# Latent attention on one Trainium2 core: turning the probabilities on VectorE and through DRAM instead of on TensorE

## The reference, cut to what matters

```python
xn = layer_norm(x, g1, b1)
ln = layer_norm(latents, g2, b2)
q = ln @ Wq
kv_input = jnp.concatenate([xn, ln], axis=1)
kv = kv_input @ Wkv
k, v = jnp.split(kv, 2, axis=-1)
q, k, v = (heads(q), heads(k), heads(v))
scale = 1.0 / np.sqrt(np.sqrt(DIM_HEAD))
logits = jnp.einsum('bhqd,bhkd->bhqk', q * scale, k * scale)
w = jax.nn.softmax(logits.astype(jnp.float32), axis=-1).astype(logits.dtype)
out = jnp.einsum('bhqk,bhkd->bhqd', w, v)
out = out.transpose(0, 2, 1, 3).reshape(b, l, INNER)
return out @ Wout
```

## Time and profile before

| | us |
|---|---|
| median of 3 runs | 1884.95 (1884.7 to 1889.27) |
| the profiled execution | 1885.37 |
| its span, first to last instruction | 1883.6 |
| PE busy / DVE / ACT / POOL in it | 1802.6 / 1199.9 / 879.5 / 616.8 |

### The profile page before, as it was taken

The page is one execution under the profiler, slowest core; times in us unless marked ns, Lnnn a source line. Parts: engine busy times, 40 slices in busy tenths (PEclk is TensorE's granted clock), DMA queues, the critical chain, the costliest instruction groups (busy, mean ns, idle before and its releaser), DMA issues. The chain is left out here.

```text
span 1883.6 us, 49778 instructions
## 1 busy us (share of the span) xinstructions
PE 1802.6 (96%) x20072; PEld 1350.2 (72%) x20072; DVE 1199.9 (64%) x2921; ACT 879.5 (47%) x1662; POOL 616.8 (33%) x744
## 2 busy tenths in 40 slices
PE   6999999999999999999999999989988999999988
PEld 4666666667888888888756667866766788888853
DVE  6677777637676666776643222238877777777767
ACT  2444444445555555555432223337764444444445
POOL 2111111103333333433313532442321444444447
PEclk9999999999999999999999999999999999999999
DMA  9300000000000000000010001321010000000001
GB/s 320 91 2 0 0 0 0 1 1 1 1 1 0 0 0 0 0 0 0 1 78 26 26 29 64 109 66 31 22 31 14 2 3 2 2 3 3 3 7 40
DMA packets 37926, 46.16 MB, mean 25 GB/s; under 512 B 5000, under 2 KB 32443, under 8 KB 37266
## 3 DMA queue, kind: packets, MB, share of 16 engines
q1 hardware_dynamic: 34450, 38.43, 6.5%
q0 software_dynamic: 3328, 5.58, 0.9%
HBM read 28.67 MB, written 17.10 MB: 24 GB/s over the span
## 5 line engine op out<-in xcount | busy, mean ns | idle before, releaser
L154 POOL TENSOR_TENSOR rstd<-var_eps,minus_half 128x2 f32<-128x2 f32 (+1 forms) x116 | 91.9, 792 | 429.5 <-DVE var_eps L148 429.4
L1068 POOL TENSOR_TENSOR xa_probs<-xa_probs,xa_total 128x512 f32<-128x512 f32 x128 | 133.0, 1039 | 196.4 <-DVE xa_total L1109 191.7
L1114 DVE TENSOR_REDUCE xa_top<-ps 128x4 f32<-128x512 f32 x128 | 88.1, 688 | 129.7 <-PE ps L933 128.4
L1029 ACT ACTIVATE xa_probs<-xa_probs 128x512 f32<-128x512 f32 x128 | 80.8, 631 | 157.2 <-DVE xa_probs L1117 157.2
L922 PEld LDWEIGHTS ps<-xa_kvT,pack_latent 128*128 128x128 f32 x512 | 97.8, 192 | 66.1 <-issue 43.8
L933 PE MATMUL ps<-xa_kvT,xa_qT 128*128 128x128 f32 x1024 | 135.2, 275 | 0.0
L949 PE MATMUL ps<-xa_probsT,xa_kv 128*128 128x512 f32 x256 | 133.2, 602 | 1.9 <-ACT xa_attnT L1038 1.8
L922 PE MATMUL ps<-xa_kvT,pack_latent 128*128 128x256 f32 x512 | 132.2, 384 | 1.4 <-PEq L343 1.4
L395 PEld LDWEIGHTS ps<-pack_moe,la_hid 128*128 128x128 f32 x1024 | 121.0, 192 | 17.4 <-issue 15.3
L382 PE MATMUL ps<-la_h2T,pack_moe 128*128 128x512 f32 x256 | 129.9, 616 | 3.3 <-ACT la_hid L591 3.3
L395 PE MATMUL ps<-pack_moe,la_hid 128*128 128x128 f32 x1024 | 125.2, 277 | 0.0
(11 more groups left out here) (355 smaller groups left out, 3954.0 us busy)
## 6 DMA issues: line engine op xcount, KB each, us to landing
expert_weights<-experts_dram SPq DMA_DIRECT2D x8, 768.0 KB, 5.9
result_pairs<-zeros SPq DMA_DIRECT2D x1, 4096.0 KB, 29.6
ca_got<-result_pairs SPq DMA_DIRECT2D x16, 256.0 KB, 2.7
slot_rows<-zeros SPq DMA_DIRECT2D x1, 2880.0 KB, 18.4
expert_rows<-slot_rows SPq DMA_DIRECT2D x8, 360.0 KB, 3.5
pack_moe<-moe_dram SPq DMA_DIRECT2D x1, 2312.0 KB
pack_latent<-latent_dram SPq DMA_DIRECT2D x1, 2050.0 KB, 15.3
pack_latent<-biased_dram SPq DMA_DIRECT2D x1, 2048.0 KB, 8.2
```

The source lines that it names most:

```text
L154: pool.tensor_tensor(m.rstd[:, 0:tiles], m.var_eps[:, 0:tiles], m.minus_half[:, 0:tiles], ALU.pow).then_inc(sem.rstd, 1)
L1068: pool.tensor_tensor(probs[:, u % 4], probs[:, u % 4], over(total[:, u % 4], 2, KEYS), ALU.mult).then_inc(probs_ready, 1)
L1114: dve.tensor_reduce(top[:, s % 4], scores, AX.X, ALU.max).then_inc(top_ready, 1)
```

## The change

The probabilities no longer go through PE. DVE transposes each 32x32 block of the probabilities' tile into `blocks`; SP stores the tile to DRAM (`turned_blocks`) and, when it has landed, loads it back with the blocks set on the keys' partitions (`probsT`). For the load's partition order to be the natural order of the keys, the scores are computed with their key columns permuted: the moving operand of `score` reads kvT with a step of 4 elements (16 bytes). Bank 2 is free, so attended values alternate between banks 2 and 3, and attending moves from slot s-3 to s-4 behind the scores.

The subtraction of the largest score is gone: the folded weights carry the factor -1/8, DVE takes the smallest of the negated scores (which is minus the largest), and ACT computes exp(-score + smallest) from PSUM straight into `probs`, in 4 instructions of 128 columns (the bias is one number per partition and pair of heads). The output projection of tiles 0 and 1 moves from slots 7 and 3 to slots 0 and 4 of the next step.

```diff
-                def copy_fold(fold, done, ready):
+                def copy_fold(fold, done, ready, scale):
...
+                            act.activation(heads[:, g, par], tiles_of(m.bank(4 + 2 * g + par)), ACT.Copy,
+                                           scale=scale).then_inc(ready, 1)
...
+            @block.sync
+            def _(sp):
+                def spread(step, u):
+
+                    sp.wait_ge(blocks_turned, count(step, UNITS, u + 1))
+                    sp.dma_start(m.turned_blocks[u % SETS].rearrange("p (j e) -> p j e", j=QUARTERS),
+                                 blocks[:, u % SETS].rearrange("p j n q -> p j (n q)")).then_inc(blocks_stored, 16)
+                    sp.wait_ge(blocks_stored, count(step, 16 * UNITS, 16 * u + 16))
+                    sp.dma_start(probsT[:, u % SETS].rearrange("p g n q -> p g (n q)"),
+                                 m.turned_blocks[u % SETS].rearrange("(g k) (j e) -> (k j) g e", g=QUARTERS, j=QUARTERS))\
+                        .then_inc(probsT_loaded[u % SETS], 16)
...
                     pe.wait_ge(q_ready, count(step, PROJ, UP * half + UP))
+                    reach(pe, exp_ready, count(step, UNITS, u - 1))
...
-                                       kvT[:, k, seq, :], start=True, stop=True)
+                                       kvT[:, k, seq, :].rearrange("p (k j) -> p j k", j=QUARTERS), start=True, stop=True)
...
-                def turn(step, u):
-                    reach(pe, probs_ready, count(step, UNITS, u + 1))
-                    reach(pe, probsT_ready, count(step, UNITS, u))
-                    for n in range(UP):
-                        mm = pe.transpose(bank(TURN_BANK)[:, P * n:P * n + P], probs[:, u % 4, n, :], w["ident"][:])
-                    mm.then_inc(probs_turned, 1)
...
+                    pe.wait_ge(probsT_loaded[u % SETS], count(step, 16 * UNITS // SETS, 16 * (u // SETS + 1)))
+                    reach(pe, attn_ready, count(step, UNITS, u - 1))
+                    pe.matmul(bank(ATTN_BANK + u % 2), kv[:, k, seq, :], probsT[:, u % SETS].rearrange("p g n q -> p n g q"),
+                              start=True, stop=True)\
...
-                            act.activation(probsT[:, u % 2], bank(TURN_BANK), ACT.Copy).then_inc(probsT_ready, 1)
...
+                            act.wait_ge(top_ready, count(step, UNITS, s + 1))
+                            reach(act, blocks_turned, count(step, UNITS, s - 3))
+                            for n in range(UP):
+                                exp = act.activation(probs[:, s % 4, n], bank(s % 2)[:, KEYS * n:KEYS * n + KEYS], ACT.Exp,
+                                                     bias=top[:, s % 4, n:n + 1], scale=-1.0)
+                            exp.then_inc(exp_ready, 1)
...
+                        if here and s >= 2 or before and s < 2:
+                            u = s - 2
+                            dve.wait_ge(probs_ready, count(step, UNITS, u + 1))
+                            reach(dve, attn_done, count(step, UNITS, u - SETS + 1))
+                            dve.transpose(blocks[:, u % SETS], probs[:, u % 4].rearrange("p n (j k) -> p j n k", k=QUARTER))\
+                                .then_inc(blocks_turned, 1)
...
-                            dve.tensor_tensor(probs[:, s % 4], scores, over(top[:, s % 4], 2, KEYS), ALU.subtract)\
-                                .then_inc(less_top, 1)
+                            dve.tensor_reduce(top[:, s % 4], scores, AX.X, ALU.min).then_inc(top_ready, 1)
```

More of the change, by code:

```diff
@@ L836, in latent_attention @@
     UP = HP // 2
+    QUARTERS = P // QUARTER
+    SETS = 4
     PROJ = HP
@@ L874, in latent_attention @@
         probs_ready = sem("probs_ready")
-        probs_turned = sem("probs_turned")
-        probsT_ready = sem("probsT_ready")
+        blocks_turned = sem("blocks_turned")
+        blocks_stored = sem("blocks_stored")
+        probsT_loaded = [sem(f"probsT_loaded_{n}") for n in range(SETS)]
         attn_done = sem("attn_done")
@@ L896, in latent_attention, with body @@
         with nc.Block() as block:
+            @block.sync
[8 more added lines that the diff above has]
+                        .then_inc(probsT_loaded[u % SETS], 16)
+                def body(step, k, ahead):
+                    for s in range(UNITS if ahead >= 0 else 2):
+                        if s >= 2 or not is_first(step):
+                            spread(step, s - 2)
+                run_steps(sp, STEPS, body, lead=LEAD)
             @block.tensor
@@ L968, in body @@
                     share = later(step, -LAG)
-                    for s in range(UNITS if ahead >= 0 else 4):
+                    for s in range(UNITS if ahead >= 0 else 5):
                         here, before = ahead >= 0, not is_first(step)
@@ L972, in body @@
                             turn_share(share)
-                        if here and s >= 2 or before and s < 2:
-                            turn(step, s - 2)
                         if here:
                             score(step, k, s)
-                        if here and s >= 3 or before and s < 3:
-                            if s == 3:
+                        if here and s >= 4 or before and s < 4:
+                            if s == 4:
                                 pe.wait_ge(kv_ready, count(step, 1, 1))
-                            attend(step, k if s >= 3 else 1 - k, s - 3)
+                            attend(step, k if s >= 4 else 1 - k, s - 4)
                         if ahead >= 1:
                             projection(later(step, 1), 1 - k, s)
-                        if s == 3 and before:
+                        if s == 0 and before:
+                            project(later(step, -1), 0)
+                        if s == 4 and before:
                             if exists(share):
@@ L1021, in body @@
                             share_rows(share)
[L1022 to L1025, removed]
-                            act.activation(probsT[:, u % 2], bank(TURN_BANK), ACT.Copy).then_inc(probsT_ready, 1)
-                        if here:
[L1028 to L1032, removed]
+                        if here:
+                            act.wait_ge(top_ready, count(step, UNITS, s + 1))
[4 more added lines that the diff above has]
+                            exp.then_inc(exp_ready, 1)
+                        if here and s >= 4 or before and s < 4:
+                            u = s - 4
                             seq, half = unit(u)
@@ L1101, in body @@
                 def body(step, k, ahead):
-                    for s in range(UNITS if ahead >= 0 else 5):
+                    for s in range(UNITS if ahead >= 0 else 6):
                         here, before = ahead >= 0, not is_first(step)
+                        if here and s >= 2 or before and s < 2:
[4 more added lines that the diff above has]
+                                .then_inc(blocks_turned, 1)
                         if here and s >= 1 or before and s < 1:
@@ L1113, in body @@
                             dve.wait_ge(scores_done, count(step, UNITS, s + 1))
[L1114 to L1119 removed]
+                            dve.tensor_reduce(top[:, s % 4], scores, AX.X, ALU.min).then_inc(top_ready, 1)
+                        if s == 5 and before:
                             dve.wait_ge(out_done, count(step, 2, 0))
```

19 lines of the change are left out of this document (7 added, 12 removed).

## The result

| us | before | after |
|---|---|---|
| median (lowest to highest) of 4 runs | 1884.83 (1874.85 to 1889.27) | 1934.8 (1932.22 to 1939.48) |
| the profiled execution, its span | 1885.37, 1883.6 | 1932.22, 1930.4 |
| scores, first to last start | 517.8 | 564.2 |
| PE / DVE / ACT busy | 1802.6 / 1199.9 / 879.5 | 1859.3 / 1201.0 / 879.9 |

The change makes the kernel slower: after over before is 1.0308, 95% interval 1.0281 to 1.0334. The forecast was 1855 us and faster. PE issues 512 instructions fewer and is busy 57 us longer.

The account below looks back on a forecast made before the run. The prediction took PE to bound the stage: 1885.4 - 56 (transposes removed) + 4 and 22 (waits) + 1 (stage's end) = 1856, less about a microsecond of old waits: 1855 us, range 1836 to 1934.

Parts of the forecast that it names:

- the price that could turn the sign: Scores' moving operand read at a 16-byte step: taken as free, 0.11 us per pass of 128 columns; at worst double.
- Rival A: Scores: the strided read slows passes to 0.20 us, about 1918 us in all, 1936 at double; waits vanish; chance 0.35.
- The removal: On PE: 32 transposes a step at 0.11 us go, 3.5 us a step, 56 us over 16 steps.
- The waits: PE waits before attending, 0.3 us a step (4 us), and before the projection for kvT, 1.6 us a step (22 us).
- The tail: Stage's end: one more slot and the DMAs, less the cover of ACT and PE's turning, cost 1 us.
- DVE's transpose: Added on DVE: one transpose of 128x512 per unit, taken at 0.69 us, between 0.49 and 1.2.
- The exponentials: Added on ACT: the exponential in 4 instructions, 1.15 us a unit instead of 0.63.
- The DMAs: Added on SP: a 256 KB store and load per unit, landing 2.3 and 2.7 us after issue, beside everything else.
- Rival B: Transpose, store and load chain is longer: about 1876 us, with several causes together 1885 to 1900; chance 0.12.
- Rival C: Nothing is late and PE runs through the stage: 1829 us, up to 1838 with small waits; chance 0.08.

Follow-up runs that it names:

- contiguous scores: The changed kernel with only the scores' moving operand read contiguously again, so keys meet wrong rows of values: 1847.38 us, ratio 0.9839 to the kernel before.
- the swap: The changed kernel with scores read contiguously and ACT reading PSUM at 16 bytes, plus slot 0's output projection issued ahead of the queries' projection: 1832.53 us, ratio 0.9754.
- the kernel with PE's write: The changed kernel with keys read contiguously and PE writing neighbouring scores 128 bytes apart in PSUM: 1853.31 us, ratio 0.9873 to the kernel before.
- the kernel with DVE's read: The changed kernel with keys read contiguously and DVE's transpose reading the probabilities in SBUF at 16 bytes: 1875.82 us, ratio 0.9954 to the kernel before.

## Why the prediction was right and wrong

- **The step that failed** is the one named as the price that could turn the sign, the term for the scores' passes, put at nothing: the 16-byte step was taken as free, because a float32 pass streams a column in only 0.86 ns and needs one stream. A pass went from 0.11 to 0.224 us, 116 us over 1024 passes against the 56 that the removal gives. The argument set PE's need against its clock; the runs show that the time per element adds: PE pays 0.88 ns for an element alone in its 16 bytes, DVE 0.79, ACT's write 0.86. Slow streaming hid nothing; why it does not, no run shows. The row of DVE was the better witness, of another engine but the same memory, and its estimate of 0.20 us lay close.
- **Rival A** at its double price, 1936 (its own terms give 1938), is what came (1934.8). Its mechanism and place are shown by two runs that take the step away or do it alone; its claim that the other waits vanish holds too, since no wait but some 4.5 us at the stage's ends is left.
- **The removal**, 32 transposes a step at 0.11 us, was right: with contiguous scores a unit is 0.89 + 0.86 + 0.87 = 2.62 us.
- **The waits** were found in the right places and a little too large: for `kvT` 1.3 us a step instead of 1.6, before attending about 0.1 instead of 0.3 in mid-stage. The output projection was the cover, as the swap shows.
- **The whole forecast but for that step**: 1855 over 1885.4 is 0.984; contiguous scores gave 0.9839. Much of this is luck, since two terms were missed that nearly cancel. I took the step for 32.6 us from first to last scores, and the sum for the same, "so PE hardly waits". But the last step lacks the queries' projections, 7 us, so that the average was too low. From one turning of the inputs to the next the trace of before has 33.26 us (679.53 to 712.79), 0.5 more than the terms add up to (32.7); in the kernel with contiguous scores it is 30.67. Those small waits went away too, some 8 us that I had not counted, and in the traces the gain is 38.5 us from first to last scores (517.8 to 479.3). Against it stands the stage's end, the next point, which costs 8.6 us there. The difference is 30 us, and the medians of the two kernels lie 31 apart.
- **The tail**, put at 1 us, was too small. From the last start of the scores to the next stage's first matmul it is 15.6 us before (940.2 to 955.8), 22.4 after (987.1 to 1009.5) and 24.2 with contiguous scores (901.5 to 925.7): PE waits for the last loads, and the last output projection stands behind these waits at a granted clock of 0.50 (from 1002 to 1006 us), 6.22 us instead of 3.81. In the traces of the whole program this is hidden, since from there to the end they have 927.8 us before and 920.9 after. The change does not touch that part, and why it got shorter is open (see the last section).

```profile
999.93 1.55 PE L966 MATMUL ps<-xa_probsT,xa_kv 128*128 128x512 f32 x2 [2.26 <-DMA xa_probsT<-turned_blocks]
1002.26 6.22 PE L975 MATMUL ps<-pack_latent,xa_attnT 128*128 128x128 f32 x32 [0.78 <-ACT xa_attnT L1052]
```

- **DVE's transpose** at 0.69 us, measured 0.706; the estimate from the Trainium skill ("VectorE: DVE Perf Modes", "The three transpose paths") of 0.71 is right as well. **The exponentials**: 1.14 us a unit as against 1.15 (the earlier trace rows give 0.27 us from start to start, not 0.26; the starts here are 0.26 apart). **The DMAs** land in 2.5 and 2.8 us against 2.3 and 2.7, and in 2.9 and 2.9 where PE runs faster.
- **Rival B** did not come: no piece of the chain was much longer. The run with attending a slot earlier shows how near it was.
- **Rival C** did not come by itself. With the step gone, the permutation in ACT's read and the projection back as cover, 0.9754 of before is reached, where its 1829 would be 0.970.

## What to carry to other kernels

When an access pattern gets a step, ask first whether two neighbouring float32 still lie in one 16-byte piece of SBUF, and price each element alone in its piece at some 0.8 to 0.9 ns, as PE's and DVE's reads and ACT's write had it here, also on an engine that streams slowly; then look whether the permutation can move to a side that is free, here ACT's read of PSUM. Put the step on the engine with slack only if nothing behind it waits: DVE's 0.4 us a unit here cost 31 of the 41 us that the change brings with a free permutation. And when an instruction moves to another place in the order, look what it covered and put another long one there.

## What the runs showed that I had not expected

- PSUM at a step is free for ACT reading (16 bytes, 368 ns) and for PE writing (128 bytes, 275 ns), while SBUF is not. The total of the kernel with PE's write is 7 us higher than this explains.
- Short waits of PE are dearer than they look. Behind waits of 1.96 and 2.18 us the granted clock stood at 0.50, the lower level, for 3 to 4 us, and an output projection of 3.73 us took 5.26; behind waits of 1.1 us it stayed at 1.00. It does not follow each time: in the kernel with DVE's read the slow projection came behind 8 of 13 waits of 1.70 to 2.00 us, and after another wait of 2.21 us in the kernel with early attending the projection took its usual 1.03 us. What decides is left open.
- Part of the traces' difference lies where the code is the same. In causal attention, far behind the changed stage, PE stands still once for 5.5 us in the kernel before and for 6.3 us in the kernel before with the step alone, at the same matmul; none of the eleven traces of the changed kernel and its variants has that halt:

```profile
PE ps L1964 <- issue: 5.5, 1, 5.5
PE ps L1964 <- issue: 6.3, 1, 6.3
```

"issue" means that the profile shows nothing that PE waited for. It is two traces on one side, and what makes the halt no run shows; but it is as large as the tail that it hides, so that a comparison of whole programs would have called the tail free.
